# A new order for the local stage, and the feed-forward layer norm by a variance product with Ln and Exp

## The chip, the core and the metric

The kernel runs on one core of one Trainium2 chip. The metric is the time of one execution on the device in microseconds; lower is better. PE is TensorE, ACT is ScalarE, DVE is VectorE, POOL is GpSimd, SP is SyncE, which issues the copies. All work on 128 partitions of SBUF and on eight PSUM banks of 512 float32 columns.

## The reference, cut to what matters

x is 4 x 1024 tokens of 128 channels. It goes through a small block attention, kept for a gate at the end, and through two layers of this:

```
def _layer(x, wqkv, qs, ksc, wo, lg, lb, w1, b1, w2, b2):
    h = shift_token(x)                       # second half of the channels from the token before
    q, k, v = split(h @ wqkv)                # 8 heads of 64
    q = l2norm(q) * qs
    k = l2norm(k) * ksc
    q, k = rotary_xpos(q, k)
    o = local_attention(q, k, v)             # windows of 64 look at themselves and the one before
    x = x + o @ wo
    h = shift_token(x)
    mu = h.mean(-1, keepdims=True)
    var = h.var(-1, keepdims=True)
    h = (h - mu) / jnp.sqrt(var + 1e-05) * lg + lb
    a, g = split(h @ w1 + b1)                # 341 each
    h = a * gelu(g)
    x = x + h @ w2 + b2
    return x
```

## The kernel before, in words

x lives transposed in SBUF: channels on partitions, 4096 tokens along the free axis (`X`). `XS` is x with the token shift; SyncE makes it by copies of halves of `X` (`copy_shifted`, L348 and L349). After the attention stage (`a_project`, `a_tile`) the function `layer` runs twice on each engine. Each engine has its own list of operations, written out in full; semaphores tie the lists together, and every wait is written by hand. Nothing reorders them, so the order in which an engine's list names its operations is the order in which they run.

The **local stage** goes over 32 tiles of 128 tokens (`local(n, par)` on each engine). A step n mixes operations of several tiles. For a tile: PE projects q, k and v (each three products of 512 columns, since the operands are split in a high and a low part); ACT squares q and k; DVE multiplies q by its tables (L1150 to L1152) and sums the squares; ACT makes 1/norm with Relu, Ln and Exp; DVE scales k (L1137) and sums q's two products (L1142, both operands in SBUF); POOL scales q, multiplies k by its tables and sums (L1359 to L1370); PE turns q and k in bank 3, ACT copies them out; PE makes masked scores in banks 4 and 5; DVE takes maxima (L1130); ACT takes exponentials with their sums (L880); DVE inverts the sums (L1116, L1170); POOL multiplies (L1348); PE turns the probabilities in bank 6, ACT copies them (L826); PE multiplies by the values; ACT copies (L831); PE multiplies by wo in bank 3; DVE adds to x (L1122). ACT copies V from bank 2 (L849). SyncE moves K's window and two halves of V to other partitions and shifts x (`back`). The input of the projections is split in a high and a low part once for four tiles, by two DVE operations of 512 columns (`split_into`, L968 and L970).

The **feed-forward stage** goes over 8 chunks of 512 tokens (`ffn(j, par)`). For a chunk: PE's mean by a product, DVE's centring (L975), ACT's squares (L899), the variance by four products with one column each (`variance`), then `rstd_links`: twelve short DVE operations of a Newton iteration for 1/sqrt on 128 x 4 numbers (L950 to L962); POOL spreads them on four diagonals (`norm_diag`, L1313), PE makes a row broadcast of them by a product with ones (`norm_bcast`), DVE multiplies (L1236), ACT and DVE split the result (L913, L1208), PE makes the hidden layer in six groups of three products, ACT the Gelu, DVE the gated product (L1217), PE the output product, DVE the addition (L1229). The first three chunks' norms stand beside the last tiles of the local stage. In layer 1 the gate with Silu follows (L918).

Of the kernel before, what the change touches and what calls it, by code (L numbers as in the profile page):

```python
# [58 lines left out]
MAGIC = float(0x5F3759DF)  # L59
# [19 lines left out]
def build(nc, a, out):  # L79
    with ExitStack() as ctx:  # L80
# [16 lines left out]
        mean_c = sb("mean_c", [P, 1])  # L97
# [24 lines left out]
        rstd = sb("rstd", [P, TILES])  # L122
        newt = sb("newt", [P, 2, TILES])
# [9 lines left out]
        V = sb("V", [P, 2, INNER])  # L133
# [17 lines left out]
        diag = qr  # L151
# [48 lines left out]
        ln_diag = sem("ln_diag")  # L200
        ln_bcast = sem("ln_bcast")
# [33 lines left out]
        l_qk = sem("l_qk")  # L235
        l_v = sem("l_v")
        l_sq = sem("l_sq")
        l_qm = sem("l_qm")
        l_norm = sem("l_norm")
# [8 lines left out]
        l_tr = sem("l_tr")  # L248
        l_tre = sem("l_tre")
# [3 lines left out]
        l_score = sem("l_score")  # L253
        l_max = sem("l_max")
        l_exp = sem("l_exp")
        l_rinv = sem("l_rinv")
        l_prob = sem("l_prob")
        l_pT = sem("l_pT")
        l_pTe = sem("l_pTe")
# [21 lines left out]
        NEWTON = 12  # L281

        def rstd_before(L, j):

            return NEWTON * (L * (CHUNKS - 1) + max(j - 1, 0))

# [21 lines left out]
        def _(sp):  # L308
# [49 lines left out]
            for L in range(DEPTH):  # L358
# [4 lines left out]

                def back(n, par):
                    nxt = 1 - par
                    base = L * TILES
                    turned, done = held(2 * (base + n + 1)), held(base + n + 1)
                    scored, pv1 = held(2 * (base + n)), held(base + n)
                    copied = held(xs_before_local(L) + 32 * (n - 2))
                    if live(n, -3, TILES):  # L370

                        sp.wait_ge(xs_dma, copied)
                    if live(n, 0, TILES):
                        sp.wait_ge(l_tre, turned)
                        wait(sp, l_score, scored)
                        sp.dma_start(kT[:, nxt, :, 0:WIN], kT[:, par, :, P:P + WIN]).then_inc(k_prev[nxt], 16)
                        sp.wait_ge(l_ve, done)
                        sp.dma_start(VB[64:P, par, :], V[0:64, par, :]).then_inc(v_prev[par], 16)
                        wait(sp, l_o, pv1)
                        sp.dma_start(VB[0:64, nxt, :], V[64:P, par, :]).then_inc(v_prev[nxt], 16)  # L380
                    if live(n, -2, TILES):
                        copy_shifted(XS[1], n - 2, P, x_before_local(L) + n - 1)

                if L == 0:

                    sp.wait_ge(zeros_made, 2)
                    sp.wait_ge(windows_zero, 1)
                    sp.dma_start(kT[:, 0, :, 0:WIN], kT[:, 1, :, P:P + WIN]).then_inc(k_prev[0], 16)
                    sp.dma_start(VB[0:64, 0, :], V[64:P, 1, :]).then_inc(v_prev[0], 16)
                steps(0, TILES + 1, back)  # L390
# [22 lines left out]
        def _(pe):  # L413
# [13 lines left out]

            def norm_bcast(n, par, base, bank):

                pe.wait_ge(ln_diag, base + n + 1)  # L430
                mm(ps[:, bank, :], ones[:], diag[:, par, :]).then_inc(ln_bcast, 1)

# [85 lines left out]
            def layer(L, tail):  # L518
# [6 lines left out]
                def project(c, hi, lo, made):  # L525

                    mm3(ps[:, c, :], hi, lo, wqkv[:, 0, c * INNER:(c + 1) * INNER],
                        wqkv[:, 1, c * INNER:(c + 1) * INNER]).then_inc(made, 1)

                def transposed(n, par, src, ready):  # L530
                    pe.wait_ge(ready, base + n + 1)
# [4 lines left out]
                def local(n, par):  # L536
# [12 lines left out]
                    def scores():  # L549
                        if live(n, 0, TILES):  # L550
# [11 lines left out]
                            for s in range(4):  # L562
                                for w, grp in ((0, 0), (1, 1), (1, 0), (0, 1)):
# [3 lines left out]
                                    if s == 3 and w != grp:  # L567
                                        last.then_inc(l_score, 1)
# [890 lines left out]
```

## Time and profile before

| | us |
|---|---|
| median of 3 runs | 908.14 (907.81 to 909.36) |
| the profiled execution: its time | 909.96 |
| its span, first to last instruction | 908.2 |
| PE busy | 800.1 (88%) |
| DVE busy | 664.4 (73%) |
| ACT busy | 654.3 (72%) |
| POOL busy | 523.9 (58%) |

The mean granted clock of TensorE is 0.972. An engine's busy share over the whole span says little here, since stages with other limits stand one behind another: the attention stage to 169 us, the local stage of layer 0 to 449, its feed-forward stage to 536, then layer 1. In rows of the timeline the first number is the start and the second the duration; what stands in brackets is the idle time before and what ended it.

### The profile page before, as it was taken

The numbers are of one execution on the slowest core, as the hardware profiler recorded it, in microseconds if no ns is written. First come the engines' busy times: TensorE is split into PE (matmuls) and PEld (weight loads), VectorE is DVE, ScalarE is ACT, GpSimd is POOL, SyncE is SP. The second block draws the span as 40 slices with busy tenths as digits, with TensorE's granted clock in tenths as the row PEclk, the third lists the DMA queues.
The fourth block names the chain that finished last, engine by engine and source line by source line (L and its number), as shares of the span: only waits on it lengthen the run. The fifth ranks groups of instructions, "written<-read, shape, count | busy, mean of one in ns | idle before, by whom it ended". The sixth has DMA issues, their size and how long they took to land.

```text
span 908.2 us, 26049 instructions
## 1 busy us (share of the span) xinstructions
PE 800.1 (88%) x9848; PEld 610.5 (67%) x9848; DVE 664.4 (73%) x1347; ACT 654.3 (72%) x2053; POOL 523.9 (58%) x521
## 2 busy tenths in 40 slices
PE   4779999779999999999989887999999999988985
PEld 1458778557777778777756545777877777775652
DVE  1577998677887787877457767778787788745765
ACT  2337777479899899889743337989988998974463
POOL 0363333078888888888511017888888888951100
PEclk8899999889999999999999998999999999999997
DMA  9110001012222222222201121222222222222001
GB/s 308 44 45 3 4 4 41 3 47 55 57 57 63 55 58 55 60 57 63 51 18 24 29 63 37 64 53 58 57 61 56 62 52 58 58 51 100 1 36 58
DMA packets 64704, 48.24 MB, mean 53 GB/s; under 512 B 40410, under 2 KB 50948, under 8 KB 64068
## 3 DMA queue, kind: packets, MB, share of 16 engines
q1 hardware_dynamic: 64580, 46.57, 19.9%
q8 instruction: 80, 1.31, 0.6%
q14 instruction: 44, 0.36, 0.1%
HBM read 10.63 MB, written 2.10 MB: 14 GB/s over the span
## 4 chain that ended last, share of the span: by engine, by line
PE 56%; ACT 17%; DVE 16%; issue 7%; POOL 1%; DMA 1%; SPq 1%; DVEq 0%; ACTq 0%; POOLq 0%
PE ps L415 47%; PE ps L425 9%; ACT prob L880 6%; DVE nmax L1130 3%; ACT sq L822 3%; DVE nt L1158 2%; ACT V L849 2%; ACT oT L831 2%; DVE split L970 2%; ACT kT L856 1%; ACT pT L826 1%; DVE prob L1217 1%; DVE split L968 1%; DMA awo<-in_awo 1%; ACT qT L841 1%
## 5 line engine op out<-in xcount | busy, mean ns | idle before, releaser
L880 ACT ACTIVATE prob<-ps,nmax 128x128 f32<-128x128 f32 x512 | 181.8, 374 | 36.7 <-DVE nmax L1130 36.7
L415 PE MATMUL ps<-wqkv,split 128*128 128x512 f32 x576 | 188.2, 438 | 14.2 <-DVE split L970 10.1
L1348 POOL TENSOR_TENSOR prob<-prob,rinv 128x512 f32<-128x512 f32 x128 | 133.9, 1046 | 88.4 <-DVE rinv L1116 45.8
L415 PEld LDWEIGHTS ps<-wqkv,split 128*128 128x128 f32 x576 | 97.5, 195 | 33.5 <-DVE split L970 10.2
L1130 DVE TENSOR_REDUCE nmax<-ps 128x4 f32<-128x512 f32 x128 | 83.6, 686 | 48.3 <-PE ps L415 48.3
L425 PE MATMUL ps<-ident,prob 128*128 128x128 f32 x640 | 98.3, 276 | 13.9 <-POOL prob L1348 13.1
L880 ACT ACTIVATION_READ_ACCUMULATOR prob<-ps,nmax 128x1 f32 x512 | 109.0, 213 | 0.0
L1359 POOL TENSOR_TENSOR qr<-qr,ss 128x512 f32<-128x512 f32 x64 | 66.9, 1046 | 53.7 <-DVE qr L1142 53.7
L425 PEld LDWEIGHTS ps<-ident,prob 128*128 128x128 f32 x640 | 76.2, 142 | 28.3 <-POOL prob L1348 17.4
L415 PE MATMUL ps<-oT,wo 128*128 128x128 f32 x512 | 73.9, 287 | 22.0 <-ACT oT L831 22.0
L826 ACT ACTIVATE pT<-ps 128x512 f32<-128x512 f32 x128 | 80.0, 625 | 10.7 <-PE ps L425 9.1
L415 PE MATMUL ps<-split,w 128*128 128x512 f32 (+1 forms) x288 | 81.4, 427 | 6.6 <-DVE prob L1217 6.3
L415 PEld LDWEIGHTS ps<-oT,wo 128*128 128x128 f32 x512 | 62.1, 191 | 37.3 <-ACT oT L831 36.3
L822 ACT ACTIVATE sq<-ps 128x512 f32<-128x512 f32 x128 | 81.8, 640 | 5.1 <-PE ps L415 5.0
L1370 POOL TENSOR_TENSOR kr<-kA,kB 128x512 f32<-128x512 f32 x64 | 82.4, 1287 | 5.0
L1364 POOL TENSOR_TENSOR kA<-kn,lrot 128x512 f32<-128x512 f32 x64 | 81.8, 1278 | 0.0
L1313 POOL TENSOR_TENSOR qr<-ident,rstd 128x512 f32<-128x512 f32 x16 | 16.6, 1042 | 99.1 <-DVE rstd L962 96.0
L415 PEld LDWEIGHTS ps<-split,w 128*128 128x128 f32 (+1 forms) x288 | 50.4, 180 | 31.1 <-DVE prob L1217 10.1
L1330 POOL TENSOR_TENSOR prob<-D,hmask 128x512 f32<-128x512 f32 x32 | 35.1, 1097 | 59.5 <-PE ps L415 59.4
L1142 DVE TENSOR_TENSOR qr<-tA,tB 128x512 f32<-128x512 f32 x64 | 68.6, 1072 | 0.0
L415 PE MATMUL ps<-pT,VB 128*64 128x64 f32 x1024 | 66.3, 228 | 1.5 <-issue 1.5
L415 PE MATMUL ps<-kT,qT 64*64 64x128 f32 x2048 | 66.8, 269 | 0.0
(139 smaller groups left out, 1871.9 us busy)
## 6 DMA issues: line engine op xcount, KB each, us to landing
VB<-V SPq DMA_DIRECT2D x129, 128.0 KB, 2.4
kT<-kT SPq DMA_DIRECT2D x65, 128.0 KB, 2.4
XS<-X SPq DMA_DIRECT2D x32, 128.0 KB, 2.3
XS<-X SPq DMA_DIRECT2D x128, 32.0 KB, 1.9
D<-in_xT SPq DMA_DIRECT2D x8, 256.0 KB, 4.4
XS<-in_xT SPq DMA_DIRECT2D x2, 1024.0 KB, 6.7
out_T<-XS SPq DMA_DIRECT2D x8, 256.0 KB, 2.0
raw<-in_wqkv SPq DMA_DIRECT2D x2, 768.0 KB, 4.4
```

Of the source, the lines that this page charges most:

```text
L415: return nc.tensor.matmul(o, l, r, start=start, stop=stop, skip_group_check=True)
L425: return nc.tensor.matmul(o, i, ident[:], is_transpose=True, start=True, stop=True, skip_group_check=True)
L822: nc.scalar.activation(sq[:, c, :], ps[:, c, :], ACT.Square).then_inc(l_sq, 1)
L826: nc.scalar.activation(pT[:, grp, :], ps[:, 6, :], ACT.Copy).then_inc(l_pTe, 1)
L880: nc.scalar.activation(prob[:, par, grp, s * P:(s + 1) * P], ps[:, 4 + grp, s * P:(s + 1) * P], ACT.Exp, bias=nmax[:, par, grp * 4 + s:grp ...
L1130: v.tensor_reduce(nmax[:, par, 4 * grp:4 * grp + 4], ps[:, 4 + grp, :].rearrange("p (s k) -> p s k", s=4), AX_X, ALU.max, negate=True).the ...
L1142: v.tensor_tensor(qr[:, nxt, :], tA[:], tB[:], ALU.add).then_inc(l_qr, 1)
L1330: g.tensor_tensor(kexp[:, par, :].rearrange("p (b h k) -> p b h k", b=BLKS, h=INGRP), part(kR, n, P).rearrange("p (b k) -> p b k", b=BLKS) ...
L1348: g.tensor_tensor(p4, p4, rinv[:, slot, 4 * grp:4 * grp + 4].unsqueeze(2).broadcast_to([P, 4, P]), ALU.mult).then_inc(l_prob, 1)
L1359: g.tensor_tensor(hd(qr[:, nxt, :]), hd(qr[:, nxt, :]), ss[:, nxt, 0:8].unsqueeze(2).broadcast_to([P, HEADS, HD]), ALU.mult).then_inc(l_qn, 1)
L1364: g.tensor_tensor(hd(kA[:]), hd(kn[:]), row8(2, pos, 0, HD), ALU.mult)
L1370: g.tensor_tensor(kr[:, nxt, :], kA[:], kB[:], ALU.add).then_inc(l_kr, 1)
```

## The change

It has two parts.

The local stage gets a new order on all engines. Each operation becomes a function of its tile (`q_projected(m)`, `k_turned(m)`, ...), and `local(n)` names them with offsets from n. Semaphores that counted two kinds of operation are split in two. The V copy moves from ACT to DVE, and V has three slots in place of two. The input split is made tile by tile, 128 columns wide (`input_high`, `input_low`). SyncE's copies get an order of their own. Steps now run from -5 on DVE and to `TILES + 2`.

The feed-forward layer norm makes the variance by one product of 512 columns with a matrix of 1/128 on all partitions, so that it is there as a broadcast; ACT then takes Ln and Exp (with -0.5) of the whole 128 x 512. The Newton links, the diagonals on POOL and the broadcast product on PE are gone. Gelu and Exp are in different tables of ACT, so `load_exp_and_ln()` stands before each in the loop.

```
-        V = sb("V", [P, 2, INNER])
+        V = sb("V", [P, 3, INNER])
...
 SyncE
                 def back(n, par):
+                    k_shifted(n)
+                    v_kept(n - 1)
+                    x_shifted(n - 3)
+                    v_shifted(n - 1)
...
 PE
                 def local(n, par):
+                    q_projected(n + 3)
+                    k_turned(n)
+                    k_projected(n + 2)
+                    probs_turned(n - 2, 1)
+                    scores(n)
+                    q_turned(n + 1)
+                    v_projected(n + 1)
+                    values_summed(n - 2)
+                    output(n - 3)
+                    probs_turned(n - 1, 0)
...
                 def variance(j, bank, slot):
                     pe.wait_ge(ln_squared, nb + j + 1)
-                    for k in range(4):
-                        last = mm(ps[:, bank, k:k + 1], sq[:, slot, k * P:(k + 1) * P], mean_c[:])
-                    last.then_inc(ln_var, 1)
+                    mm(ps[:, bank, :], mean_w[:], sq[:, slot, :]).then_inc(ln_var, 1)
...
                 local(TILES, 0)
+                bias_products()
+                local(TILES + 1, 1)
+                local(TILES + 2, 0)
                 variance(2, 2, 0)
-                pe.wait_ge(ln_rstd, rstd_before(L, 0) + 1)
-                norm_bcast(0, 0, nb, 0)
-                local(TILES + 1, 1)
-                norm_bcast(1, 1, nb, 1)
...
                     if live(j, 3, CHUNKS):
-                        wait(pe, ln_scaled, fb + j + 2)
+                        pe.wait_ge(ln_log, nb + j + 3)
                         mean(j + 3, 0)
...
 ACT
                 def local(n, par):
+                    k_squared(n + 2)
+                    probs_copied(n - 2, 1)
+                    q_squared(n + 3)
+                    norm_floor(n + 2)
+                    q_copied(n + 1)
+                    norm_log(n + 2)
+                    norm_inverse(n + 2)
+                    exponentials(n, 0)
+                    exponentials(n, 1)
+                    probs_copied(n - 1, 0)
+                    k_copied(n + 1)
+                    o_copied(n - 2)
...
+                def inverse_deviation(j, bank):
+                    act.wait_ge(ln_var, nb + j + 1)
+                    wait(act, ln_rstd, nb + j - 1)
+                    nc.scalar.activation(lnlog[:, j % 2, :], ps[:, bank, :], ACT.Ln, bias=floor[:, 2:3]).then_inc(ln_log, 1)
+                    act.wait_ge(ln_log, nb + j + 1)
+                    wait(act, ln_scaled, nb + j - 1)
+                    nc.scalar.activation(rstd[:, j % 2, :], lnlog[:, j % 2, :], ACT.Exp, scale=-0.5).then_inc(ln_rstd, 1)
...
                         for c, (u, n) in enumerate(PARTS):
+                            if c == 2 and live(j, 3, CHUNKS):
+                                load_exp_and_ln()
+                                inverse_deviation(j + 3, 0)
...
                 local(TILES + 1, 1)
+                act.wait_ge(l_trq, base + TILES)
+                for j in range(3):
+                    inverse_deviation(j, j)
...
 DVE
+                def input_high(m):
+                        wait(dve, l_v, base + m - 2 * TPC + 1)
+                        v.tensor_copy(split[:, (m // TPC) % 2, 0, bass.ds((m % TPC) * P, P)],
+                                      shifted(XS[0], m, P)).then_inc(split_hi, 1)
...
+                def v_copied(m):
+                        dve.wait_ge(l_v, base + m + 1)
+                        wait(dve, l_o, base + m - 2)
+                        if base + m >= 2:
+                            dve.wait_ge(v_prev[m % 2], 32 * ((base + m - 2) // 2 + 1))
+                        v.tensor_copy(V[:, (base + m + 1) % 3, :], ps[:, 2, :]).then_inc(l_ve, 1)
...
                 def local(n, par):
+                    inverse_sums(n - 2, 1)
+                    input_high(n + 5)
+                    inverse_sums(n - 1, 0)
+                    v_copied(n)
+                    q_rotated(n + 2)
+                    input_low(n + 5)
+                    q_summed(n + 2)
+                    k_summed(n + 2)
+                    maxima(n, 0)
+                    maxima(n, 1)
+                    q_sin(n + 3)
+                    q_cos(n + 3)
+                    k_scaled(n + 2)
+                    added_to_x(n - 3)
...
                 centre(nb, 1, shifted(XS[1], 1, CHUNK), 1)
                 local(TILES - 1, 1)
-                inverse_sums(TILES - 1, 1)
+                local(TILES, 0)
                 ffn_weights(L)
-                links(0, 1, NEWTON, 0, 2)
                 centre(nb, 2, shifted(XS[1], 2, CHUNK), 2)
                 ffn_bias(L)
-                add_to_x(TILES - 2)
+                local(TILES + 1, 1)
...
+                local(TILES + 2, 0)
                 scaled(0, tA)
...
 POOL
                 def local(n, par):
+                    k_cos(n + 2)
+                    k_sin(n + 2)
+                    normalised(n, 0)
+                    k_rotated(n + 2)
+                    normalised(n, 1)
+                    q_scaled(n + 3)
```

## Rows read from the trace of the kernel before

**Rows 1.** Timeline: the first score matmuls of the first and last tile, both layers.

```profile
188.78 0.41 PE L415 MATMUL ps<-lmask,ident_bf 64*64 64x512 bf16 x4
...
445.08 0.41 PE L415 MATMUL ps<-lmask,ident_bf 64*64 64x512 bf16 x4
...
549.27 0.53 PE L415 MATMUL ps<-lmask,ident_bf 64*64 64x512 bf16 x4
...
806.55 0.41 PE L415 MATMUL ps<-lmask,ident_bf 64*64 64x512 bf16 x4
```

**Rows 2.** Busy time by stage: us, PE, PEld, DVE, ACT, POOL, PEclk, DMA share, GB/s.

```profile
189.00:445.00 256.00, 233.39 (x3072) 189.73 (x3064) 198.58 (x376) 231.50 (x830) 214.57 (x216) 0.99 0.24 57
...
462.00:530.00 68.00, 63.97 (x238) 40.65 (x238) 44.92 (x115) 23.39 (x35) 5.21 (x5) 0.97 0.10 24
```

**Rows 3.** Timeline of PE in one step without a split.

```profile
571.63 0.97 PE L415 MATMUL ps<-wqkv,split 128*128 128x512 f32 x3
...
577.42 1.16 PE L415 MATMUL ps<-oT,wo 128*128 128x128 f32 x8 [0.39 <-ACT oT L831]
...
579.59 0.50 PE L415 MATMUL ps<-wqkv,split 128*128 128x512 f32 x1
```

**Rows 4.** Busy time of the engines over about one such step.

```profile
572.00:580.00 8.00, 7.61 (x103) 6.30 (x102) 6.21 (x13) 7.59 (x30) 7.03 (x8) 1.00 0.25 59
```

**Rows 5.** Timeline of DVE and POOL around one input split.

```profile
593.22 0.74 POOL L1366 TENSOR_TENSOR kB<-kn,lrot 128x256 f32<-128x256 f32 x1
...
593.55 0.69 DVE L968 CAST split<-XS 128x512 fp32r<-128x512 f32 x1
...
594.04 1.34 POOL L1370 TENSOR_TENSOR kr<-kA,kB 128x512 f32<-128x512 f32 x1
594.28 1.65 DVE L970 TENSOR_TENSOR split<-XS,split 128x512 fp32r<-128x512 f32 x1
```

**Rows 6.** Timeline of the feed-forward stage: first Gelu, and two broadcast products.

```profile
463.77 1.28 ACT L908 ACT_TABLE_LOAD   x1
...
465.06 0.69 ACT L908 ACTIVATE kA<-ps,bias 128x512 f32<-128x512 f32 x1
...
485.31 0.59 PE L415 MATMUL ps<-qr,ones 128*128 128x512 f32 x1
...
494.68 0.59 PE L415 MATMUL ps<-qr,ones 128*128 128x512 f32 x1
```

**Rows 7.** Costliest groups of the page: busy us, mean ns of one | idle before.

```profile
L1348 POOL TENSOR_TENSOR prob<-prob,rinv 128x512 f32<-128x512 f32 x128 | 133.9, 1046 | 88.4 <-DVE rinv L1116 45.8
...
L1130 DVE TENSOR_REDUCE nmax<-ps 128x4 f32<-128x512 f32 x128 | 83.6, 686 | 48.3 <-PE ps L415 48.3
...
L826 ACT ACTIVATE pT<-ps 128x512 f32<-128x512 f32 x128 | 80.0, 625 | 10.7 <-PE ps L425 9.1
...
L1364 POOL TENSOR_TENSOR kA<-kn,lrot 128x512 f32<-128x512 f32 x64 | 81.8, 1278 | 0.0
```

**Rows 8.** Durations in ns (min/median/max) by tile: qr, split and XS.

```profile
L1142 DVE TENSOR_TENSOR qr<-tA,tB x64: 681/1065/1207, 180.0 to 794.6; 128x512 f32<-128x512 f32 x64
...
L968 DVE CAST split<-XS x16: 414/674/696, 169.2 to 759.0; 128x512 fp32r<-128x512 f32 x16
L970 DVE TENSOR_TENSOR split<-XS,split x16: 691/1648/1656, 169.6 to 759.7; 128x512 fp32r<-128x512 f32 x16
...
L1322 POOL TENSOR_TENSOR XS<-tA,tB x8: 1278/1670/1676, 28.8 to 64.4; 128x512 f32<-128x512 f32 x8
```

**Rows 9.** The same for X: a DVE operation of 128 columns.

```profile
L1122 DVE TENSOR_TENSOR X<-X,ps x64: 271/289/289, 209.3 to 820.9; 128x128 f32<-128x128 f32 x64
```

**Rows 10.** Timeline of layer 0: DVE's feed-forward weights, the first feed-forward matmuls.

```profile
450.19 0.55 DVE L1095 TENSOR_SCALAR w<-raw,vecs 128x682 fp32r<-128x682 f32 x1
...
450.77 1.58 DVE L1097 SCALAR_TENSOR_TENSOR w<-raw,vecs,w 128x682 fp32r<-128x682 f32 x1
...
461.98 3.06 PE L415 MATMUL ps<-split,w 128*128 128x512 f32 x12
```

More of the change, by code:

```diff
@@ L361, in _ @@
                     load_attn(L + 1)
-                def back(n, par):
[L365 to L382, printed above, removed]
+                base = L * TILES
@@ new lines, in probs_turned, with output @@
+                def probs_turned(m, grp):
+                    if 0 <= m < TILES:
+                        pe.wait_ge(l_prob[grp], base + m + 1)
+                        wait(pe, l_pTe[1 - grp], base + m + grp)
+                        for s in range(4):
+                            last = turn(ps[:, 6, s * P:(s + 1) * P], prob[:, m % 2, grp, s * P:(s + 1) * P])
+                        last.then_inc(l_pT[grp], 1)
+                def output(m):
+                    if 0 <= m < TILES:
+                        if m == 0:
+                            pe.wait_ge(wo_in, 16 * (L + 1))
+                        pe.wait_ge(l_oe, base + m + 1)
+                        if 0 <= m + 4 < TILES:
+                            pe.wait_ge(l_tq, base + m + 4 + 1)
+                        elif 0 <= m + 3 < TILES:
+                            pe.wait_ge(l_tk, base + m + 3 + 1)
+                        elif 0 <= m - 1 < TILES:
+                            pe.wait_ge(x_new, x_before_local(L) + m - 1 + 1)
@@ new lines, in exponentials @@
+                def exponentials(m, grp):
+                    if 0 <= m < TILES:
+                        act.wait_ge(l_max[grp], base + m + 1)
+                        for s in range(4):
+                            col = slice(grp * 4 + s, grp * 4 + s + 1)
+                            nc.scalar.activation(prob[:, m % 2, grp, s * P:(s + 1) * P],
+                                                 ps[:, 4 + grp, s * P:(s + 1) * P], ACT.Exp, bias=nmax[:, m % 2, col],
+                                                 accum_out=rsum[:, m % 2, col]).then_inc(l_exp[grp], 1)
@@ new lines, in local @@
+                def local(n, par):
+                    k_squared(n + 2)
[10 more added lines that the diff above has]
+                    o_copied(n - 2)
@@ L1196, in layer @@
                 gate = L + 1 == DEPTH
-                def links(j, first, last, bank, chunks=1):
-                    if first == 1:
-                        dve.wait_ge(ln_var, nb + j + chunks)
-                    variances = ps[:, bank, 0:4] if chunks == 1 else ps[:, bank:bank + chunks, 0:4]
-                    rstd_links(variances, j, 4 * chunks, rstd_before(L, j), first, last)
                 def lows(j, slot, t):
@@ L1390, in shape_constants @@
+                steps(-3, TILES - 1 + 0, local)
 def shape_constants():
```

611 lines of the change are left out of this document (284 added, 327 removed).

## The prediction

> **What bounds the kernel now.** I read the granted clock first, then stretches by stage, then the timeline of one step of the local stage on all engines, then the groups of instructions of the engines that share work. The time is 908.2 us of span in a run of 909.96, with a median of 908.14, so a difference in span can be taken as a difference in the median. The local stage, 32 tiles in each of two layers, is the bulk of it. From the first score matmul to the last there are 256.3 us in layer 0 (445.08 - 188.78) and 257.3 in layer 1 (806.55 - 549.27) [rows 1], so 8.27 and 8.30 us for each of 31 steps, at a granted clock of 0.99 [rows 2]. TensorE's clock is at its upper level of 2.4 GHz there and has nothing to give.
>
> One ordinary step takes 7.96 us, from one q projection to the next [rows 3]. In a window of 8.00 us PE is busy 7.61, ACT 7.59, POOL 7.03 and DVE 6.21 [rows 4]. In PE's step the only wait of size is 0.39 us for ACT's copy of the previous output [rows 3]. So PE and ACT are both nearly full, and the step is long because ACT's list is. 31 ordinary steps would be 246.8 us. The 9.5 us that are left are seven steps with an input split and the last step, in which two mean products stand before the tile. Rows 5 show what a split costs: the cast starts on DVE while POOL computes, takes 0.69, and the subtraction behind it takes 1.65 and holds back the second maximum, and all engines follow. The feed-forward loop has a period of 9.37 us (494.68 - 485.31) [rows 6], and PE is busy 63.97 of 68.0 us in that stage [rows 2]: it is PE's.
>
> **Part 1: the local stage in a new order.** It moves the bank copy of V from ACT to DVE, cuts the input split into four 128-column pieces, one each tile, and puts each operation in the step where its input is ready (q two tiles and a half ahead, the probabilities and the output later). The matmuls and their shapes stay. I put one step together for each engine.
>
> *PE.* 7.96 less the wait of 0.39 is 7.57, and a few waits of hundredths go with it: 7.5 us. This is the floor of a step.
>
> *ACT.* 7.59 busy less one bank copy. The nearest is the copy of the turned probabilities, 0.63 us [rows 7]. That leaves 7.0. It still has to wait for two turned tiles per step, with some 0.5 us of room for it.
>
> *DVE.* 6.21 busy, in which a sum of q takes 1.07 because it waits for POOL, against 0.68 alone [rows 8]. It gains the V copy; the trace has none, so it is bounded by nothing below (no engine copies a bank at no cost, so half of 0.69 is the least) and by the reduction of a whole bank, 0.69 [rows 7], above. I take 0.61, for neighbours overlap. The pieces of the split are 128 wide. A 128-wide operation lasts 0.29 [rows 9]; alone the 512-wide ones take 0.41 and 0.69 [rows 8]. I take 0.13 and 0.21 a tile after overlap, with 0.6 each as the upper bound. 6.21 - 0.39 (the wait for POOL in the q sum) + 0.61 + 0.34 = 6.8, and some 0.3 less once operations that stood alone stand side by side and overlap: 6.5 us with no wait for POOL in it.
>
> *POOL.* 7.03 of 8.00 us [rows 4]: three products of 1.05, one of 1.28, two of 0.74 and a sum of 1.3 [rows 5, 7], overlapping by hundredths, about 6.9 to 7.0.
>
> *What they take from each other.* The cast started 0.41 us before POOL's product ended at 593.96 and finished 0.28 after it; the subtraction started at 594.28 and ran 0.55 beyond the end of POOL's sum at 595.38 [rows 5]. Its shortest is 0.69, its median 1.65 [rows 8]. The other way round, POOL's sum in the attention stage takes 1.67 in place of 1.28 when such a DVE operation runs [rows 8]. So the two engines do not run a DVE operation with two SBUF operands (or this cast) and a POOL product together: the later one waits. With POOL idle for 0.9 us a step this is free for POOL now. In the new order it is not: POOL must step aside for the q sum (0.55), the subtraction (a quarter, 0.15) and the cast (0.07), together 0.8. 6.9 + 0.8 = **7.7 us**. DVE comes to nearly the same: 6.5, and up to 0.3, 0.2 and 1.0 of waiting for the POOL product that runs when each of the three is due, 7.5 to 8.0. Both lie above PE's 7.5, so I take 7.7 for the step, with 7.5 below and the present 7.96 above.
>
> The Trainium skill (SBUF — State Buffer, section "Who interferes with whom") says that the second of two such instructions blocks until the first has finished, and counts casts in a two-port mode and DVE operations with both inputs in SBUF among them. The trace agrees [rows 5]. A model of shared bandwidth would give 7.5 and some 12 us less in all.
>
> Layer 0: 31 x 7.7 = 238.7, plus 2.0 for the two mean products (now wholly on a PE without spare time) and 1.0 until the pipeline is full, 241.7 against 256.3: **-14.6**. Layer 1: 241.7 against 257.3: **-15.6**. POOL is what is late next.
>
> *SyncE.* The same five copies per tile, in a new order. In it, K's copy waits for the turned k; V's for DVE's copy of one tile earlier; x's for the addition of three tiles earlier. What is queued behind x is the shifted V copy, which PE needs more than a step later, and V has a third buffer. I cost this at nothing; its cover is that step, and if it is gone each tile pays a copy.
>
> **The drain.** The order is deeper by one tile, and that has to be paid after the last scores. Before, the first feed-forward matmul is 16.9 us behind them (461.98 - 445.08) [rows 1, 10]. After, PE turns tile 30's second probabilities only behind two variance products and a mean, at about +6.7 from the last scores. Turn and copy (about 0.6 each), value products and output product (about 1.1 each, as the 1.16 of [rows 3]) put tile 29's addition to x at +10.6. Then DVE does the feed-forward weights, 0.55 and 1.58 [rows 10], a centring and the bias before it may invert the last sums, +13.8. From there in series: POOL's product 1.05 [rows 7], turn, copy, value products, output product and addition of tile 30, output product and addition of tile 31, +20.3. ACT begins its logs at +18.1, and the third waits for the last variance: five bank operations and two splits more, and the first feed-forward matmul is at about +23.6. That is **+6.75** a layer, **+13.5** in all; bounds +3 (if DVE's weights find a gap) and +9 a layer. The fill of layer 1 loses about **+1.0**: the second q projection now stands before the first k projection on PE and waits for DVE, which is behind the previous layer's last hidden products.
>
> **Part 2: the layer norm.** It removes 12 short DVE links, POOL's diagonal, and a broadcast product on PE for each chunk: the row of 0.59 is one of its two passes, 0.43 from one to the next, so 0.86 [rows 6]. The variance becomes a 512-column product, two such passes, in place of eight loads and products of about 1.0: nothing gained or lost. ACT gains Ln and Exp of a bank, 0.63 each [rows 7], and two table loads of 1.28 [rows 6], 3.8 us, for five chunks a layer. PE's period falls from 9.37 to some 8.9. But ACT's loads now lie in a ring: hidden product on DVE, centring, squares, two Gelus, load, Ln, Exp, load, Gelu, high copy, low part on DVE, next hidden product. With operations of 0.6 to 0.7 and two loads that is 9.05. So a period is shorter by 0.3 only, and the first chunk is slower by 1.7, as the ring starts empty. In layer 0 the last chunk's low part is no longer behind the broadcast, 1.0 earlier: -0.65 in total. In layer 1 the Silu of the gate adds another load inside the ring at one chunk, +1.3: +1.35 in total. Together **+0.7**; bounds -6 (PE's period throughout) and +8 (ACT's list the ring from chunk to chunk with one more load in four of them).
>
> **Sum.** -14.6 - 15.6 + 13.5 + 1.0 + 0.7 = -15.0: 908.1 - 15 = **893 us**.
>
> **Rivals.**
> *PE stays the bound, 7.5 a step.* POOL's and DVE's claims fall where the other is idle. For it: DVE's copies from PSUM do not touch POOL (the reductions are 0.69 at POOL's side as elsewhere). Against: only 0.5 us of POOL's step would be free. 62 x 0.2 = 12.4 less: 881.
> *ACT's list still sets the step, 7.93.* Moving V does not help if the two turned tiles come late to ACT in the new order. Then only the splits are won: 62 x 0.23 = 14 more: 907, no change.
> *DVE is shut out (the slower side).* POOL's products follow each other with no gap in the new order, and rows 5 show a DVE operation let in only where POOL had a pause behind it (593.96 to 594.04). If POOL's next product keeps the way, the q sum waits for one product more, 1.05, every tile, and everything behind it on DVE: the reductions, maxima, ACT's exponentials. 62 x 1.05 = 65: 958. It decides from 0.24 us a step on (15 / 62), so a quarter of the tiles is enough.
> *A table load costs about twice its row.* If an unseen emptying of the engine belongs to each, as long as the load, ten chunks pay 2 x 1.28 more: +26, 919. Against it: the load follows the squares at once, and the Gelu follows it.
> The Trainium skill (ScalarE: Activation LUTs, "What ACT_TABLE_LOAD costs") gives such a drain, 1.38 us beside the 1.28 of the load, and by it the ten chunks would cost 27.6 us more. The trace shows 1.28 and nothing around it [rows 6].
>
> **How the numbers follow.** Forecast 0.45, its own range 884 to 904 (a step of 7.6 to 7.85, the drain by 3 either way). PE the bound 0.20. ACT's list 0.10. DVE shut out, wholly or in part, 0.18. Table loads 0.03. Something unseen 0.04. The range that leaves 2 in 10 out is 876 to 914. A measurement of this kernel tells 0.2%, 1.8 us, from no change. Faster takes the first two, a third of ACT's case and some of DVE's small end: 0.73. The same 0.06, slower 0.21.
>
> **What would show it.** Right: steps without a split step among them, 7.7 from one q projection to the next; POOL busy over 90% with its products longer than 1.05 here and there; q sums of 1.0 and low pieces near 1 us on DVE; 22 to 24 us from the last scores to the first feed-forward matmul; periods of 9.05 with ACT rows of two loads. Wrong: PE with waits over 0.5 us a step, a wait of V's projection or of the value products for a copy of SyncE, or a drain no longer than before.

## The result, and the profile after

The changed kernel takes 883.87 us (883.27 to 884.41, 4 runs) against 908.65 (907.81 to 909.36) beside it: ratio 0.9731, 95% interval 0.9717 to 0.9746. The forecast was 893. The time lies inside the range from 876 to 914, but it came about by another sum than mine. All ratios are of fast executions; of the ten of E2 below, one took 2559.93 us and is left out of its ratio.

Busy times of the changed kernel, from the page:

```profile
PE 787.1 (89%) x9720; PEld 595.3 (68%) x9720; DVE 682.5 (77%) x1338; ACT 669.7 (76%) x2041; POOL 531.5 (60%) x505
```

The first score matmuls of the first and last tile of both layers, from the timeline (they answer to [rows 1]):

```profile
192.23 0.41 PE L422 MATMUL ps<-lmask,ident_bf 64*64 64x512 bf16 x4
...
421.44 0.41 PE L422 MATMUL ps<-lmask,ident_bf 64*64 64x512 bf16 x4
...
537.85 0.64 PE L422 MATMUL ps<-lmask,ident_bf 64*64 64x512 bf16 x4
...
768.12 0.41 PE L422 MATMUL ps<-lmask,ident_bf 64*64 64x512 bf16 x4
```

Stretches by stage (columns as in [rows 2]): the local stage of layer 0, its drain, the feed-forward stage with the fill of layer 1, and two pieces of lower clock in them, the late drain and the fill:

```profile
192.23:421.44 229.21, 223.03 (x3025) 182.19 (x3024) 217.48 (x442) 216.66 (x797) 223.22 (x213) 1.00 0.27 63
421.44:446.45 25.01, 18.87 (x204) 14.36 (x203) 6.87 (x18) 12.78 (x34) 3.44 (x4) 0.86 0.16 37
446.45:537.85 91.40, 76.71 (x243) 45.79 (x243) 53.01 (x90) 49.68 (x70) 9.18 (x9) 0.92 0.13 32
...
430.00:446.00 16.00, 11.14 (x92) 8.61 (x87) 4.69 (x12) 7.66 (x13) 1.04 (x1) 0.79 0.09 22
518.00:538.00 20.00, 12.86 (x39) 8.35 (x43) 17.28 (x32) 5.46 (x14) 9.33 (x9) 0.71 0.22 53
```

Cut at the same events in every kernel (first scores; last scores; first feed-forward matmul; the first of DVE's three hidden products of the last chunk; next first scores; end), the spans divide like this, in us. "Drain" is the way from the last scores of a layer to its first feed-forward matmul, "fill" the way from the feed-forward stage of layer 0 to the first scores of layer 1. E1 to E12 are the experiments below.

| | before 1st scores | local 0 | drain 0 | FFN 0 | fill 1 | local 1 | drain 1 | FFN 1 | end |
|---|---|---|---|---|---|---|---|---|---|
| before | 188.8 | 256.3 | 16.9 | 71.7 | 15.6 | 257.3 | 16.9 | 70.4 | 14.4 |
| changed | 192.2 | 229.2 | 25.0 | 70.8 | 20.7 | 230.3 | 25.3 | 72.7 | 15.6 |
| E1 order alone | 191.3 | 228.8 | 30.2 | 71.8 | 20.5 | 228.8 | 28.2 | 71.7 | 15.6 |
| E2 norm alone | 188.8 | 257.0 | 16.3 | 72.2 | 14.3 | 256.2 | 16.2 | 72.9 | 15.5 |
| E3 new drain | 192.3 | 229.4 | 16.9 | 70.1 | 20.4 | 230.0 | 16.9 | 76.3 | 14.6 |
| E4 low part later | 190.4 | 229.3 | 25.0 | 64.6 | 20.1 | 230.2 | 25.2 | 65.6 | 15.6 |
| E10 E3 and E4 | 192.5 | 229.3 | 16.9 | 65.0 | 20.4 | 229.2 | 16.9 | 66.0 | 15.5 |
| E11 fastest | 191.4 | 229.2 | 16.9 | 62.8 | 18.2 | 230.1 | 16.9 | 62.8 | 12.9 |

The local stages won 54.1 us, and half of it was given back: 16.5 in the drains, 5.0 in the fill, 3.4 ahead of the first scores, 2.5 in the feed-forward stages and the end. (The spans of the two profiled executions differ by 26.6 us, the medians by 24.8.) The 3.4 is not all the change's: E3, E4, E10 and E11 have the same operations there, and their first scores lie between 190.4 and 192.5.

An ordinary step is now 7.39 us from score matmul to score matmul, all but the first and last few alike. One such step, as a window:

```profile
300.00:307.39 7.39, 7.39 (x103) 6.13 (x102) 7.33 (x16) 7.15 (x28) 7.38 (x8) 1.00 0.28 65
```

PE, DVE and POOL are all full, and busy time cannot say which of them sets the step. A busy time holds waits too: a DVE or POOL operation that waits for the other shows as one long operation. DVE and POOL in it, from the timeline:

```profile
299.49 1.04 POOL L1375 TENSOR_TENSOR prob<-prob,rinv 128x512 f32<-128x512 f32 x1
...
300.17 0.90 DVE L1171 TENSOR_TENSOR qr<-tA,tB 128x512 f32<-128x512 f32 x1
300.49 1.49 POOL L1382 TENSOR_TENSOR qr<-qr,ss 128x512 f32<-128x512 f32 x1
301.00 1.13 DVE L1142 TENSOR_TENSOR split<-XS,split 128x128 fp32r<-128x128 f32 x1
301.94 1.32 POOL L1390 TENSOR_TENSOR kA<-kn,lrot 128x512 f32<-128x512 f32 x1
302.05 0.67 DVE L1177 TENSOR_REDUCE nt<-sq 128x8 f32<-128x512 f32 x1
```

Read it as a queue for one door, through which one of the two engines goes at a time. DVE's q sum is due at 300.17, waits for POOL's product to end at 300.53, and runs its 0.54. POOL's next product stands in line behind it and shows 1.49 in place of 1.04. DVE's low part is due at 301.00, comes second, and shows 1.13 where its shortest is 0.29; POOL's next, at 301.94, loses only 0.04. Each operation is late by what is left of the other's, and which engine pays depends on who came first.

### The profile page after: what moved, and what is told of

Read it like the earlier page. It is cut to its first block and busy times, and to the rows that moved or that the text cites. A ratio compares the mean times of both kernels' runs of the same rounds, so it can differ in the third digit from the quotient of the medians.

```text
span 881.6 us, 26513 instructions
## 1 busy us (share of the span) xinstructions
PE 787.1 (89%) x9720; PEld 595.3 (68%) x9720; DVE 682.5 (77%) x1338; ACT 669.7 (76%) x2041; POOL 531.5 (60%) x505
## 5 line engine op out<-in xcount | busy, mean ns | idle before, releaser
L899 ACT ACTIVATE prob<-ps,nmax 128x128 f32<-128x128 f32 x512 | 179.3, 375 | 2.7 <-DVE nmax L1196 2.7
L1382 POOL TENSOR_TENSOR qr<-qr,ss 128x512 f32<-128x512 f32 x64 | 92.0, 1437 | 118.3 <-ACT ss L892 118.3
L422 PE MATMUL ps<-split,w 128*128 128x512 f32 (+1 forms) x288 | 87.7, 447 | 15.9 <-DVE prob L1262 14.2
L1196 DVE TENSOR_REDUCE nmax<-ps 128x4 f32<-128x512 f32 x128 | 81.6, 677 | 11.8 <-PE ps L422 11.5
L1390 POOL TENSOR_TENSOR kA<-kn,lrot 128x512 f32<-128x512 f32 x64 | 84.2, 1316 | 0.9 <-DVE kn L1189 0.9
L422 PEld LDWEIGHTS ps<-split,w 128*128 128x128 f32 (+1 forms) x288 | 51.4, 183 | 48.4 <-DVE prob L1262 20.4
L422 PE MATMUL ps<-oT,wo 128*128 128x128 f32 x512 | 76.7, 294 | 0.9 <-DVE X L1210 0.9
L422 PEld LDWEIGHTS ps<-pT,VB 128*64 128x64 f32 x1024 | 53.1, 140 | 25.8 <-issue 25.8
L422 PEld LDWEIGHTS ps<-oT,wo 128*128 128x128 f32 x512 | 64.3, 197 | 5.8 <-issue 1.5
L422 PE MATMUL ps<-pT,V 128*64 128x64 f32 x1024 | 64.7, 225 | 0.0
L422 PEld LDWEIGHTS ps<-kT,qT 64*64 64x64 f32 x2048 | 61.1, 134 | 4.7 <-issue 0.2
```

The source lines that it names most:

```text
L422: return nc.tensor.matmul(o, l, r, start=start, stop=stop, skip_group_check=True)
L899: nc.scalar.activation(prob[:, m % 2, grp, s * P:(s + 1) * P], ps[:, 4 + grp, s * P:(s + 1) * P], ACT.Exp, bias=nmax[:, m % 2, col], accum ...
L1196: v.tensor_reduce(nmax[:, m % 2, 4 * grp:4 * grp + 4], ps[:, 4 + grp, :].rearrange("p (s k) -> p s k", s=4), AX_X, ALU.max, negate=True).t ...
L1382: g.tensor_tensor(hd(qr[:, m % 2, :]), hd(qr[:, m % 2, :]), ss[:, (base + m) % 2, 0:8].unsqueeze(2).broadcast_to([P, HEADS, HD]), ALU.mult ...
L1390: g.tensor_tensor(hd(kA[:]), hd(kn[:]), row8(2, m, 0, HD), ALU.mult)
```

## The experiments

### What sets the step (E5 to E9)

E5, E6 and E7 each take work from one engine of the changed kernel, E8 moves an operation and E9 builds on E6. All five are read at the step, the median from one first score matmul to the next. Each was run once: 883.31 us (E5), 876.39 (E6), 880.25 (E7), 880.17 (E8) and 854.27 (E9).

E5, POOL:

```
-                        g.tensor_tensor(hd(qr[:, m % 2, :]), hd(qr[:, m % 2, :]), ss[... 0:8] ..., ALU.mult)
+                        half = hd(qr[:, m % 2, :])[:, 0:HEADS // 2, :]
+                        g.tensor_tensor(half, half, ss[... 0:4] ..., ALU.mult)
```

> The changed kernel; POOL scales only the first four heads of q (the other four stay unscaled), so that its product is 256 columns and some 0.5 us shorter. If POOL and its waits for DVE set the step of 7.39 us, it falls to 6.9. If DVE's list sets it by itself, also less than 7.39 but only by what DVE waits for that product at the low part (0.9 us at present): 6.9 as well. If PE's list sets it (no idle of size is to be seen on PE either): 7.3 to 7.4 and no change.

E6, PE, in `project`:

```
-                    mm3(ps[:, c, :], hi, lo, w_hi, w_lo)
+                    mm(ps[:, c, :], hi, w_hi, True, False)
+                    mm(ps[:, c, :], lo, w_hi, False, True)
```

> The changed kernel without the third product of each projection in the local stage (the low part of the weights is left out), three products of 512 columns less on PE per tile, some 0.8 us. If PE sets the step: 6.7 to 7.0. If POOL and DVE set it, as the prediction had it: 7.39 as before, and PE shows 0.7 us of waits a step.

E7, DVE:

```
-                        v.tensor_tensor(split[:, slot, 1, cols], shifted(XS[0], m, P), split[:, slot, 0, cols] ..., ALU.subtract)
+                        v.memset(split[:, slot, 1, cols].bitcast(F32), 0.0)
```

> The changed kernel with the low part of the input set to zero by a memset in place of the subtraction, so that DVE has no operation there that must wait for POOL's product (0.9 us of its 1.12). If DVE's list with that wait sets the step: 6.6 to 6.9, or the next engine's floor. If POOL sets it: POOL wins only 0.05 us or so, 7.30 to 7.39. If PE: 7.39.

The same stretch of E5, E6 and E7, in this order, as windows (us, PE, PEld, DVE, ACT, POOL, clock, DMA share, GB/s):

```profile
260.00:390.00 130.00, 130.00 (x1769) 108.13 (x1765) 123.55 (x265) 123.80 (x462) 122.38 (x123) 1.00 0.27 63
```

```profile
260.00:390.00 130.00, 127.75 (x1735) 95.73 (x1736) 129.61 (x266) 124.53 (x459) 130.00 (x125) 1.00 0.29 66
```

```profile
260.00:390.00 130.00, 130.00 (x1775) 107.79 (x1774) 115.10 (x263) 123.54 (x456) 129.16 (x124) 1.00 0.28 65
```

The steps are 7.39 in E5, 7.35 in E6 and 7.39 in E7. With POOL at 94% (E5) or DVE at 89% (E7) nothing changes, so neither of them sets the step of 7.39, and by E8 below, where ACT's list is fuller and the step the same, ACT does not either. PE is left, and E6 fits: with three products of 512 columns less on PE the step falls, but by 0.04 only, so that neither of the values expected for E6 came. Now POOL has no gap: POOL, with what it loses at the door, needs 7.35. The two limits lie 0.04 apart. PE is found by exclusion, and a ring of waits through PE would look the same in these runs.

DVE is nearly full in E6 as well, but it is not what holds it, since its q sum still has to wait for POOL. It is due at 305.31, POOL's product ends at 305.64, and the sum shows 0.88:

```profile
304.60 1.04 POOL L1376 TENSOR_TENSOR prob<-prob,rinv 128x512 f32<-128x512 f32 x1
...
305.31 0.88 DVE L1172 TENSOR_TENSOR qr<-tA,tB 128x512 f32<-128x512 f32 x1
305.60 1.50 POOL L1383 TENSOR_TENSOR qr<-qr,ss 128x512 f32<-128x512 f32 x1
```

PE's busy time says little here. It fell from 130.00 to 127.75 in 130 us, 0.13 a step, though three products a step were gone, and the profile lists no wait of PE in E6.

E8 undoes one part of the change, V's copy on DVE:

```
-                    v_copied(n)               (DVE, 4th of its list)
+                    v_copied(n + 1)           (ACT, between k_copied(n + 1) and o_copied(n - 2))
```

> The changed kernel with the copy of V back on ACT, behind the copy of k. ACT is busy 6.99 us of 7.39 a step and would be at 7.6, DVE gets 0.57 free. If ACT then sets the step: 7.6 to 7.9, 890 to 900 us. If it does not (its list overlaps more): 7.39 and 882 to 885.

The step stayed at 7.39, with ACT at 129.46 of 130 us. The one run took 880.17, 3.7 us less than the changed kernel and outside both expectations; E12 takes that up. The same stretch as a window:

```profile
260.00:390.00 130.00, 130.00 (x1776) 107.87 (x1775) 127.93 (x246) 129.46 (x476) 129.91 (x124) 1.00 0.28 64
```

E9 is E6 with a q sum of a quarter of the width, so that POOL has less to wait for while PE is out of the way. (E6 leaves out the low part of the weights, E9 also three quarters of q's sum.)

```
-                        v.tensor_tensor(qr[:, m % 2, :], tA[:], tB[:], ALU.add)
+                        v.tensor_tensor(qr[:, m % 2, 0:P], tA[:, 0:P], tB[:, 0:P], ALU.add)
```

> The kernel of the step with two products per projection, and q's sum on DVE over 128 of its 512 columns (the rest of q keeps old numbers). With PE's work cut the step was 7.35 with POOL busy throughout, q's scaling on POOL lasting 1.49 in place of 1.04 behind the q sum. If POOL gives that time up because DVE's sum holds the memory for its own 0.5 us, the scaling now lasts 1.1 to 1.2 and the step is 7.0. If the 1.49 has another cause (the scaling's own operands): 7.35 again.

Durations of the scaled q on POOL (min/median/max in ns) in the changed kernel and in E9:

```profile
L1382 POOL TENSOR_TENSOR qr<-qr,ss x64: 1043/1492/1503, 182.3 to 758.0; 128x512 f32<-128x512 f32 x64
```

```profile
L1384 POOL TENSOR_TENSOR qr<-qr,ss x64: 1042/1093/1106, 181.1 to 729.2; 128x512 f32<-128x512 f32 x64
```

In E6 the median is 1.492 as well. The step fell from 7.35 in E6 to 6.94. POOL's product is the same in both; only the DVE operation ahead of it became shorter. DVE has 0.4 less to do by it too, but in E6 it was waiting for POOL. So the 0.4 was time that POOL gave DVE. Of the 6.94, 0.05 and 0.04 are still lost to the short q sum and the low part, so that POOL's own list is some 6.85 us (an estimate from these rows). The step of 6.94 also shows that PE, with two products a projection, can go at least 0.45 faster than 7.39.

### The two parts apart (E1, E2)

> The new local order alone, with the feed-forward layer norm of before (Newton links, diagonals, broadcast product). In the profile of the changed kernel the two local stages are 54.1 us shorter from first to last scores, the first scores 3.5 later, the two drains 8.1 and 8.4 longer and the way from the last hidden product of layer 0 to the first scores of layer 1 5.1 longer. If these all belong to the local order and the norm adds only what its feed-forward stages show (-0.9 and +2.3), this kernel is 1 to 3 us below the changed one: 881 to 884. Rival: the long drain is the doing of Ln and Exp, three in a row behind the last output copy; then the drains here are near the 16.9 of before and the time is 866 to 870.

> The variance product with Ln and Exp alone, with the local order of before. If the norm is nearly neutral, as its feed-forward stages in the changed kernel say (-0.9 in layer 0, +2.3 in layer 1, drains within 2 us of before): 907 to 913, first feed-forward matmul 16 to 19 us behind the last scores. Rival: it costs the drains 6 to 8 us each: 922 or more.

E1 took 888.25 us, ratio 0.9785 (0.9771 to 0.9800); E2 910.22, ratio 1.0023 (1.0011 to 1.0034). Both expectations for E1 fell. The long drain belongs to the order, since E2 has 16.3, but with the Newton links it is longer still, 30.2. Two rows of E1 show a part of why:

```profile
434.87 0.16 DVE L1241 RECIPROCAL rinv<-rsum 128x4 f32<-128x4 f32 x1
435.11 1.04 POOL L1439 TENSOR_TENSOR prob<-prob,rinv 128x512 f32<-128x512 f32 x1 [9.04 <-DVE rinv L1241]
```

Twelve links stand in DVE's list ahead of that inverse. The inverse comes 14.8 us behind the last scores there and 12.4 in the changed kernel, which is some 2.4 of the 5.2 us that E1's drain is longer; the rest was not followed. So Ln and Exp in place of the Newton links cost 2.6 us in the old order (910.22 against 907.58 beside it) and save 4.4 in the new one (883.87 against 888.25): a part's worth depends on the list it stands in. E2 and the changed kernel have twenty table loads more than the kernel before (33 against 13), and E2's two feed-forward stages are 0.5 and 2.5 us longer.

### The drain (E3)

DVE, POOL and PE in the changed kernel's drain, from the timeline (in brackets the idle time before):

```profile
431.46 0.29 DVE L1210 TENSOR_TENSOR X<-X,ps 128x128 f32<-128x128 f32 x1 [6.09 <-PE ps L422]
...
433.86 0.16 DVE L1203 RECIPROCAL rinv<-rsum 128x4 f32<-128x4 f32 x1
434.10 1.04 POOL L1375 TENSOR_TENSOR prob<-prob,rinv 128x512 f32<-128x512 f32 x1 [6.67 <-DVE rinv L1203]
...
435.19 1.12 PE L432 MATMUL ps<-ident,prob 128*128 128x128 f32 x4 [2.24 <-POOL prob L1375]
...
439.06 2.08 PE L422 MATMUL ps<-oT,wo 128*128 128x128 f32 x8
```

The sums of tile 31 are there at 426.4, where ACT's last exponential ends, and inverted at 433.86: `inverse_sums(TILES - 1, 1)` stands behind `added_to_x(TILES - 3)`, which waits 6.09 us for PE, and behind the feed-forward weights and the third centring. The order of before had it ahead of them.

```
 DVE
-                local(TILES - 1, 1)
-                local(TILES, 0)
-                ffn_weights(L)
...
+                maxima(TILES - 1, 1)
+                inverse_sums(TILES - 1, 0)
+                added_to_x(TILES - 4)
+                inverse_sums(TILES - 1, 1)
+                ffn_weights(L)
+                centre(nb, 2, shifted(XS[1], 2, CHUNK), 2)
+                added_to_x(TILES - 3)
...
 ACT
+                o_copied(TILES - 3)
+                inverse_deviation(0, 0)
+                probs_copied(TILES - 1, 0)
...
 PE
+                probs_turned(TILES - 1, 0)
+                values_summed(TILES - 2)
+                output(TILES - 3)
+                probs_turned(TILES - 1, 1)
+                bias_products()
+                values_summed(TILES - 1)
```

> The changed kernel with only the last steps of the local stage put in another order: on DVE the inverse of the last two tiles' sums before the additions to x that wait for PE, and the feed-forward weights and third centring in the gap; on PE the turns of tile 31 before output products, on ACT the first Ln and Exp in the gap. If the drain is long because DVE's list holds back the inverses (POOL stood idle 6.67 us for rinv), it falls from 25.0 to 14 to 17 us a layer, PE's clock does not fall in it, and the time is 862 to 868. Rival: PE's work at the lower granted clock and the serial chain of tile 31 set it anyway; then at most 3 us a layer are won, 878 or more.

It took 865.81 us, ratio 0.9535 (0.9501 to 0.9570). The drain is 16.9 in both layers, and the inverse comes at 427.61:

```profile
421.00:438.00 17.00, 15.77 (x205) 12.61 (x205) 7.26 (x16) 12.61 (x35) 4.33 (x5) 1.00 0.22 51
...
427.61 0.18 DVE L1219 RECIPROCAL rinv<-rsum 128x4 f32<-128x4 f32 x1 [1.99 <-ACT prob L904]
427.70 0.55 DVE L1122 TENSOR_SCALAR w<-raw,vecs 128x682 fp32r<-128x682 f32 x1
427.87 1.28 POOL L1399 TENSOR_TENSOR prob<-prob,rinv 128x512 f32<-128x512 f32 x1 [1.31 <-DVE rinv L1219]
...
431.98 0.60 PE L432 MATMUL ps<-ident,prob 128*128 128x128 f32 x4
...
434.68 1.16 PE L422 MATMUL ps<-oT,wo 128*128 128x128 f32 x8
```

The granted clock stays at 1.00, 2.4 GHz, where the changed kernel had 0.79 from 430 to 446, part of the time at 1.2 GHz: the turn took 1.12 there in place of 0.60 and the output product 2.08 in place of 1.16. In the changed kernel's drain PE is busy 18.87 of 25.01 us, in E3 15.77 of 17.00. E3's feed-forward stage of layer 1 is 3.6 us longer than the changed kernel's, at a granted clock of 0.91 against 0.98. This may be a matter of the execution that was profiled: E3's four took 868.48 (the profiled one), 868.42, 862.72 and 863.20, at mean clocks of 0.964, 0.964, 0.974 and 0.972. Why the clock differs among them stays open.

```profile
775.80:852.10 76.30, 67.34 (x206) 39.66 (x204) 34.45 (x53) 57.94 (x72) 0.00 (x0) 0.91 0.11 43
```

### The feed-forward ring (E4, E10, E11, E12)

The first period of the stage in the changed kernel:

```profile
453.48 1.28 ACT L949 ACT_TABLE_LOAD   x1
454.78 0.68 ACT L949 ACTIVATE kn<-ps,bias 85x512 f32<-85x512 f32 x1
455.36 0.62 ACT L954 ACTIVATE split<-tA 128x512 fp32r<-128x512 f32 x1
456.08 0.69 DVE L1253 TENSOR_TENSOR split<-tA,split 128x512 fp32r<-128x512 f32 x1 [7.97 <-ACT split L954]
456.69 0.75 DVE L1262 SCALAR_TENSOR_TENSOR prob<-ps,bias,kA 128x512 f32<-128x512 f32 x1
...
457.49 3.53 PE L422 MATMUL ps<-split,w 128*128 128x512 f32 x9 [2.82 <-DVE prob L1262]
```

DVE waits 7.97 us for ACT's high copy, to make a low part that nobody needs before the chunk after next, and the hidden product that PE needs next stands behind it. E4 moves the low part:

```
 DVE, ffn(j, par)
                     if live(j, 3, CHUNKS):
                         centre(nb, j + 3, shifted(XS[1], j + 3, CHUNK), 0)
+                    if 1 <= j and j + 1 < CHUNKS:
+                        lows(j + 1, 1 - par, tA)
                     hidden(1)
...
-                        lows(j + 2, par, tA)
```

> The changed kernel with the low part of chunk j+2 on DVE moved behind the first hidden product of chunk j and the centring, so that no product waits for ACT's list of two table loads. If that ring sets the period of 9.05 us, the first period falls from 11.0 to 9 or less and the others to PE's own 8.5: 4 us a layer, 874 to 878. Rival: PE's list is the period already (busy 19.3 of 20 us); then only the first period gains, 880 to 883.

It took 866.48 us, ratio 0.9547 (0.9524 to 0.9569), 17 us and not 8 less than the changed kernel. The two feed-forward stages are 6.2 and 7.1 us shorter in the profile, where I had expected 4 each. The steady period went from 9.11 to 8.68, near to what was expected. What I had not counted lies elsewhere. In layer 0 the first hidden product is 3.8 us behind the first feed-forward matmul in place of 10.2; the second follows it after 13.05 in place of 10.22, so that 3.6 us of this are kept. The fifth period fell from 8.55 to 7.21. In layer 1 the first two keep 2.5, and the fourth period, in which the gate with Silu and its own table load begin, fell from 11.80 to 8.69. The profiled spans differ by 15.7; 1.8 of it lies ahead of the first scores, where the edit changes nothing.

E10 is E3 and E4 together.

> The new drain and the feed-forward low part behind the first hidden product, both together. If the two gains are independent (-18.1 and -17.4 against the changed kernel, each measured by itself): 848 to 850. If part of each was the same time, such as the wait of the first chunk behind the drain: 852 to 858.

E11 puts `lows(j + 1, 1 - par, tA)` behind `hidden(2)`, and for layer 1:

```
 PE
-                    steps(-3, -2, local)
+                    q_projected(0)
+                    k_projected(0)
                     tail(CHUNKS, 0)
+                    q_projected(1)
 ACT
+                    k_squared(0)
+                    norm_floor(0)
+                    norm_log(0)
+                    norm_inverse(0)
+                    q_squared(1)
 DVE, for local(-2, 0)
+                    k_summed(0)
+                    k_scaled(0)
+                    q_sin(1)
+                    q_cos(1)
```

> The same, with the low part behind the third hidden product in place of the first, and in layer 1 k's projection, squares and norm of tile 0 ahead of q's of tile 1. In the changed kernel PE waits 3.88 us for q's cosine product between the last hidden product and the first scores, 20.65 us in all. If that serial chain sets the fill: 14 to 17 us, and with 2 us off the first feed-forward period of each layer 840 to 845. If the hidden products and the clock set it: within 2 us of the kernel without.

E10 took 851.46 us, ratio 0.9366 (0.9340 to 0.9393): 18.1 and 17.4 less than the changed kernel would be 848.4, so the two gains add up but for 3.1 us. The four executions of E10 lie between 847.99 and 853.33, so that it cannot be said whether the 3.1 is real. E11 took 843.17, ratio 0.9288 (0.9274 to 0.9302), as expected, though not for the reason expected. The feed-forward stages are 2.1 and 3.2 us shorter with a period of 8.51, the end 2.6, and the fill, at which the edit was aimed, only 2.3, to 18.2 where 14 to 17 was expected. The 2.6 of the end is PE's clock: its last six matmuls take 5.49 us in E10 and 2.84 in E11. Why the clock is higher there was not tested. The end of E10 and of E11 as windows:

```profile
836.00:851.50 15.50, 5.49 (x6) 1.85 (x6) 8.64 (x13) 1.26 (x2) 0.00 (x0) 0.55 0.18 68
```

```profile
828.30:841.20 12.90, 2.84 (x6) 1.06 (x6) 8.60 (x13) 1.26 (x2) 0.00 (x0) 0.81 0.22 81
```

In E11 PE still waits in the fill:

```profile
510.05 2.90 PE L422 MATMUL ps<-wqkv,split 128*128 128x512 f32 x6 [3.39 <-DVE tA L1182]
```

E12 is E11 with the edit of E8.

> The fastest kernel so far (new drain, low part behind the hidden products, k's chain first in layer 1) with the copy of V on ACT in place of DVE. With V on ACT in the changed kernel the steps stayed at 7.39 us and one run was 3.7 us shorter. If PE sets the step and the copy is free on either engine: the same as without within 0.3%, 841 to 845. If ACT's fuller list makes the exponentials late here, where it has no slack of 0.4 us left: 846 or more. If the 3.7 us were real, from DVE's shorter lists at the ends of the stages: 838 to 840.

E12 took 844.86 us, ratio 0.9298 (0.9283 to 0.9314). Its interval and that of E11 overlap, and both profiles have a local stage of 229 to 230 us. All four of its executions (844.61 to 845.60) lie above those of E11 (842.15 to 844.19), but the ratios to the kernel before, each measured beside its own, differ by 0.001 only. So no gain is to be seen with V's copy on ACT, and no cost clear of the noise; the 3.7 us of the one run of E8 did not come again.

## Why the prediction was right or wrong

| term | predicted | measured |
|---|---|---|
| local stage 0 with what is ahead of it | -14.6 | -27.1 + 3.4 |
| local stage 1 | -15.6 | -27.0 |
| fill of layer 1 | +1.0 | +5.0 |
| drains | +13.5 | +8.1 + 8.4 |
| feed-forward stages and the end | +0.7 | -0.9 + 2.3 + 1.1 |
| sum (spans) | -15.0 | -26.6 |

**The step failed.** "I take 7.7 for the step", and "POOL is what is late next": both were wrong. The step is 7.39 and PE sets it, as the first rival said. Two sizes were off.

The first is what POOL gives up. Its own list was nearly right, 6.85 (from E9) against 6.9. But I let it step aside for 0.8 us, the full length of all three DVE operations. It loses 0.45 to the q sum and about 0.04 to the low part, since there DVE comes second and pays itself. That gives 7.34, and E6 shows 7.35.

The second is PE's floor of 7.5, which was 0.11 too high. I had taken the idle time of 0.39 [rows 3] out of the old step of 7.96. (The median step was 7.93.) But around that wait the scores and the output product took 1.04 and 1.09 us from their start to where the next operation starts or the wait begins. In the changed kernel, without a wait, they take 0.97 and 0.99:

```profile
575.99 1.04 PE L415 MATMUL ps<-kT,qT 64*64 64x128 f32 x32
577.42 1.16 PE L415 MATMUL ps<-oT,wo 128*128 128x128 f32 x8 [0.39 <-ACT oT L831]
578.51 0.34 PE L415 MATMUL ps<-pT,VB 128*64 128x64 f32 x4
```

```profile
301.89 1.04 PE L422 MATMUL ps<-kT,qT 64*64 64x128 f32 x32
302.86 0.66 PE L432 MATMUL ps<-ident,qr 128*128 128x128 f32 x4
...
305.23 1.16 PE L422 MATMUL ps<-oT,wo 128*128 128x128 f32 x8
306.22 0.60 PE L432 MATMUL ps<-ident,prob 128*128 128x128 f32 x4
```

So the wait may have cost PE some 0.17 more than the idle time listed. The operations that follow are others in the new order, and it was not tested.

62 steps by 0.31 are 19 us, of the 23.9 by which the two local stages came out shorter than predicted. The rest is the 3.0 a layer that I had added for the mean products and the start. In layer 0 the last step takes 9.47, 2.1 more than the others, as foreseen, but the first three (6.33, 7.32, 7.09) and the two before the last (6.96, 7.25) are shorter and make up for it; in layer 1 1.2 of it is left.

That the rival's 881 is nearer to 883.87 than my 893 is partly luck, and so is it that 883.87 lies only just below the forecast's own range of 884 to 904. With the right step and all my other terms the sum is 874. The drains, the fill and the stretch ahead of the first scores, 3.0, 4.0 and 3.4 us longer than I had them, brought it back up.

**The lock was right**, and so were its consequences in the trace: q sums of 0.9, low pieces of 1.13, products of 1.49. The Trainium skill (SBUF — State Buffer, "Who interferes with whom") says that whoever issues first has the ports for the whole instruction. E9 agrees: with a shorter DVE operation ahead of it POOL's product falls from 1.49 to 1.09. What I made of it was wrong: it does not say that POOL pays each time.

**ACT's list and the V copy.** "The step is long because ACT's list is" was wrong in its cause. E8 gives ACT the same operations as before and holds them in 7.39 us, busy 129.46 of 130. Not the length of ACT's list set the old step but the order of the lists, and the V copy had no part in the gain (E8, E12). The rival that ACT would still set the step fell with it.

**DVE shut out** fell as well, at 0.18 the case that I feared most: in the steady steps DVE's q sum shows 0.88 to 1.11 and never the 1.05 more of one product longer, so DVE got in at each boundary between two POOL products, with no pause needed.

**The drain** was right in kind and 3 us too small: +6.75 against +8.1 and +8.4. The mechanism was named ("DVE does the feed-forward weights ... before it may invert the last sums"). The inverse came at +12.4 and not at +13.8; the chain behind it took 12.6 us where I had 9.8. Missing was the clock at its lower level for part of the last 16 us. What I did not see is that it was avoidable (E3).

**The fill** was 4 us too small. PE waits 3.88 us and then 3.39 for q products of DVE, again at a lower clock, 0.71. E11 won 2.3 of it; what sets the rest stays open.

**The feed-forward part** was right in its mechanism: 9.11 and not 9.05 for the ring's period, the first chunk slower, -0.9 and +2.3 us in the two stages against -0.65 and +1.35. A table load costs its row and nothing beside it: in the rows above the Gelu starts 0.02 behind the end of the load, and twenty loads more, with all else that comes with them, cost E2 2.6 us in the median. The Trainium skill (ScalarE: Activation LUTs, "What ACT_TABLE_LOAD costs") would have the 27.6 us more; neither E2's time nor the ring's period, 0.06 from a sum with 1.28 for each load, shows them.

## What to carry to other kernels

When several engines are all full after a change, take work from one at a time and look at one step: here two limits lay 0.04 us apart, and neither busy times nor waits could name the first. An order made for the steady state has to be written anew for its last tiles. In an in-order list, an operation whose input waits for another engine's long list must not stand ahead of one that somebody needs now: two such places, one in the drain and one in the feed-forward ring, cost 16.5 and 13.3 us by their stages, and with them and a smaller edit put right the kernel takes 843.17 us.

## What the hardware showed

DVE and POOL take turns instruction by instruction, and a DVE operation gets in between two POOL products that stand back to back (299.49 to 301.94 above). In the drain PE ran part of the time at 1.2 GHz, which the turn behind an idle time of 2.24 us is the first to show, and its matmuls in the serial chain took near to twice as long there (1.12 in place of 0.60, 2.08 in place of 1.16); in E3, without that idle time, the same matmuls ran at 2.4 GHz.
